# Where TensorE takes a pair's shared-expert down product within an even step

## The reference, cut to what matters

```python
x  = x + attention(layernorm(x), ctx)                  # Wq, Wk, Wv, Wout, bout
xn = layernorm(x)
logits = (xn @ Wr) / 16                                # 8 experts
idx = top_k(logits + rb, 2)                            # two experts for a token
w   = softmax(logits taken at idx)
routed = sum over idx of w * ((xn @ W1[e]) * silu(xn @ W3[e])) @ W2[e]     # H = 512
shared = ((xn @ Ws1) * silu(xn @ Ws3)) @ Ws2                               # H = 512
out = x + routed + shared
```

## Time and profile before

| what | value |
|---|---|
| median of 3 runs | 1096.32 us (1096.11 to 1097.06) |
| the profiled execution's own time | 1097.37 us |
| its span | 1095.3 us |
| mean granted TensorE clock | 0.985 |
| PE busy | 1061.2 us (97%) |
| DVE, POOL, ACT busy | 743.3 (68%), 705.3 (64%), 694.3 us (63%) |

### The profile page before, as it was taken

One profiled execution on the slowest core, in us unless ns is written; L12 is line 12 of the kernel. 1 busy time (PEld: TensorE's weight loads), 2 busy tenths in 40 slices (PEclk: granted clock), 3 DMA queues, 4 the chain that ended last, 5 costly groups with the idle time before them and its releaser, 6 DMA issues. The chain is left out here.

```text
span 1095.3 us, 25507 instructions
## 1 busy us (share of the span) xinstructions
PE 1061.2 (97%) x7342; PEld 929.1 (85%) x7342; DVE 743.3 (68%) x1940; ACT 694.3 (63%) x1649; POOL 705.3 (64%) x658
## 2 busy tenths in 40 slices
PE   6999999999999999999999899999999999999996
PEld 4788888888888888888887799999888888888886
DVE  5788888888888888888888676656443333433332
ACT  6888888888888888888886554332334343343442
POOL 4988889888988888898887556555033223332233
PEclk9999999999999999999998999889999999999998
DMA  8014431442144214421532295223473354333861
GB/s 247 17 41 131 139 103 37 139 139 94 45 139 139 86 53 139 139 78 62 178 103 94 77 304 185 81 76 127 147 217 56 58 137 87 56 56 62 269 176 15
DMA packets 83985, 124.06 MB, mean 113 GB/s; under 512 B 7904, under 2 KB 48080, under 8 KB 83920
## 3 DMA queue, kind: packets, MB, share of 16 engines
q1 hardware_dynamic: 63664, 99.86, 28.0%
q0 software_dynamic: 11760, 15.15, 7.7%
q10 hardware_dynamic: 8496, 8.22, 2.6%
HBM read 74.44 MB, written 49.68 MB: 113 GB/s over the span
## 5 line engine op out<-in xcount | busy, mean ns | idle before, releaser
L559 POOL TENSOR_TENSOR probs<-probs,first_rows 112x750 f32<-112x750 f32 x128 | 184.0, 1438 | 66.1 <-DVE first_rows L1019 64.9
L1801 POOL DMA_INDIRECT out<-stage,to_row x48 | 74.9, 1560 | 175.7 <-ACT stage L1853 114.6
L2082 DVE TENSOR_TENSOR hT_lo<-banks,hT_hi 128x512 fp32r<-128x512 f32 x63 | 43.6, 692 | 185.3 <-ACT hT_hi L1845 179.4
L753 ACT ACTIVATE probs<-banks,first_rows 112x375 f32<-112x375 f32 x256 | 145.8, 573 | 18.2 <-DVE first_rows L1006 16.0
L1006 DVE TENSOR_REDUCE first_rows<-banks 112x2 f32<-112x750 f32 x128 | 119.6, 934 | 26.1 <-PE banks L1391 24.4
L519 POOL TENSOR_TENSOR v_both<-v_raw,v_both 125x512 fp32r<-125x512 f32 x96 | 123.7, 1288 | 7.5
L1012 DVE TENSOR_TENSOR pT<-banks,pT 125x672 fp32r<-125x672 f32 x128 | 108.8, 850 | 18.2 <-ACT pT L744 17.0
L1405 PEld LDWEIGHTS banks<-pT,v_both 125*128 125x128 f32 x768 | 99.7, 192 | 17.4 <-issue 10.4
L1405 PE MATMUL banks<-pT,v_both 125*128 125x224 f32 x768 | 110.9, 280 | 2.2 <-DVE oT_lo L1037 1.7
L515 POOL TENSOR_TENSOR v_both<-v_raw,one 125x512 fp32r<-125x512 f32 x96 | 110.6, 1152 | 0.1
L1417 PE MATMUL banks<-ident,probs 112*125 112x112 f32 x768 | 107.6, 277 | 1.4 <-POOL probs L559 0.7
(11 more groups left out here) (286 smaller groups left out, 3066.6 us busy)
## 6 DMA issues: line engine op xcount, KB each, us to landing
w_split_scratch<-stage SPq DMA_DIRECT2D x16, 1536.0 KB, 6.6
ring<-w_split_scratch SPq DMA_DIRECT2D x16, 1536.0 KB
stage<-in_L_ffn_W SPq DMA_DIRECT2D x48, 256.0 KB, 3.0
ctx_in<-in_ctx SPq DMA_DIRECT2D x32, 376.0 KB, 3.8
xg<-x_sorted_scratch ACTq DMA_DIRECT2D x59, 136.0 KB
x_in<-in_x SPq DMA_DIRECT2D x16, 224.0 KB, 3.3
x_res<-in_x SPq DMA_DIRECT2D x32, 112.0 KB, 2.1
x_scratch<-x SPq DMA_DIRECT2D x32, 112.0 KB, 1.9
```

The costliest lines, as they stand in the source:

```text
L559: pool.tensor_tensor(probs[:, two, :], probs[:, two, :], inv_sum[:, 2 * s:2 * s + 2].rearrange("p (e o) -> p e o", o=1).to_broadcast([N, 2 ...
L753: act.activation(probs[:, h % 4, :], S_BANKS[0:N, e, 0:M], ACT.Exp, bias=neg_max[:, h:h + 1], accum_out=row_sum[:, h:h + 1]).then_inc(exp_ ...
```

## The change

On PE, in the even steps 2 to 24, `down_shared` moves from the end of the step to right behind `up1`, and so ahead of turn_block, turn_rows, router, ranks and the read of the ring's place. In step 26 it stays where it was. No instruction is added or removed, and no other engine's list changes.

```diff
                 if g < LAST:
                     up1(g)
+                if 2 <= g < SHARED_FIRST and g % 2 == 0:
+                    down_shared(g // 2 - 1)
                 j = g + 2 - SHARED_FIRST
                 if 0 <= j < BLOCKS:
                     turn_block(j)
@@
                     ring_off[n] = pe.value_load(ring_at[0:1, n:n + 1], min_val=0, max_val=2 * SLOT)
-                if 2 <= g <= SHARED_FIRST and g % 2 == 0:
+                if g == SHARED_FIRST:
                     down_shared(g // 2 - 1)
```

## The result

The change made the kernel slower: 1100.70 us in the median of 20 runs (1095.38 to 1104.26) against 1095.62 for the kernel before in 20 runs (1092.88 to 1101.71), a ratio of 1.0037 with a 95% interval of 1.0025 to 1.0048. Single executions of either kernel scatter by some 9 us, far more than the three runs shown before had suggested. The profiled execution took 1099.61 us with a span of 1097.5; its partner before took 1097.37.

What follows compares the result with a forecast made beforehand. PE, busy 1061.2 of 1095.3 us, was taken to bound the kernel. The terms -1.35 - 2.7 + 0.7 = -3.35 us took the median from 1096.32 to 1093.0 us, with an 8-in-10 range of 1089.5 to 1097.3.

Steps and rivals of the forecast that it cites:

- (a): PE's waits in steps 4, 10, 16 and 24: work resumes earlier with the new order, -1.35 us, bounds 0 and 3.25.
- my sign: Check in the changed profile: steps 4, 10, 16 idle about 0.7 us ahead of the down product, until ACT's `hi`.
- (b): Granted clock in the shared steps: three of five open falls after thin products remain, -2.7 us, bounds 0 and -7.9.
- Moved past: Steps 6 and 12: rows turned 2.9 us later, 0.8 us in hand where there were 3.7; given no term.
- (c): POOL's transfers run without a gap and hold PE's signals back in steps 6 and 12: +0.7 us, bounds 0 and +5.9.
- What POOL loses by the later start it has in hand: POOL's later start of slots and transfers costs nothing, since it waits for the next statistics after each chunk.
- The slower rival: Router of steps 7 and 13 waits behind held signals and the clock falls: 5.9 us more, 1098.9 us, chance 0.15.
- Its deciding point: Router waits if signals come free over 0.8 us after the turning's end; step 6 was put at 0.5 us.
- The clock rival: Clock falls as before in the shared steps, five falls making 9.4 us, (b) is 0: 1095.7 us, chance 0.26.

## Why the prediction was wrong, step by step

**(a) The waits, -1.35 us: failed.** The router's waits went, as forecast, but the down product's were 1.79, 1.01 and 0 us in steps 4, 10, 16, where my sum left 0.69, 0.45 and 0.34 (and my sign said 0.7 each): 2.8 us of idle time for 2.56. I took ACT's `hi` from the trace of before as a fixed time. It can itself stand behind a held signal. In the profile after, chunk 0's eight transfers ran in one train until 651.66, and the down product of step 4 started at 651.52. That train was not closed by the change, as shown above, so the 1.79 us are in part the draw of this execution. In step 24 the wait was 0.43 us, ahead of the down product, where it had been 0.69 us ahead of the turning; the separate run of that step found no gain.

**(b) The clock, -2.7 us: failed for the whole change, half right for the part it was argued for.** The mean granted clock is 0.9875 after (20 runs) and 0.9870 before (76 runs of the experiments, on four chips, whose means go from 0.9858 to 0.9876): no gain that can be told. With steps 4, 10, 16 alone it is 0.9895 (12 runs), against 0.9876 for the kernel before on the same chip (33 runs). Within kernels a run has some 0.83 us less for each 0.001 of granted clock (a fit over all runs, its scatter 1.6 us), so that part seems to have gained some 1.6 us by the clock, and as its time did not move, lost as much elsewhere; its profile has 1.1 us more idle time (7.4 against 6.3 in the stretch), and the rest is not shown. The full change did not keep the clock's gain: with the later turning alone it is 0.9868, and in the profile after three of the four falls stand right behind the waits of steps 4, 13 and 19, the fourth in step 5 behind thin products without a wait. That the falls of one trace are one draw held: they came at other places in every trace, and the runs scatter by 9 us. I wrote that one trace cannot tell and still built a sum with terms of 1 to 3 us on it.

**Moved past, the later turning of rows in steps 6 and 12, put at nothing: the step that decided the sign.** I counted 0.8 us in hand of the 3.7 there had been and gave it no term. Moved alone, these two steps cost 1.0045, some 5 us, and steps 4, 10, 16 alone cost nothing that can be told (1.0007). With the same closed trains, the kernel without the later turning has 1.0008 and the whole change 1.0037. My reading is that the slack let PE bear held signals: in step 13 they came 4.0 us after the turning, with 0.8 us in hand. Where no train is longer than five, the later turning costs nothing either (0.9905 against 0.9903). So in this change it took both, and I had priced them apart.

**(c) POOL's transfers close up, +0.7 us: right in kind and too small.** The mechanism is the one in the text: long trains hold PE's signals back, and breaking them up takes the loss away. In chunk 1 the six in a row came as forecast, and PE lost nothing there. The loss came from what I had not seen. I had trains of six; those of chunks 3 and 5 ran eight, since `hid` of two steps on was ready as well and the second gate was open too. I charged PE only for its short stops (0.45 us), not for what waits behind the signals: the router in step 13 and the ranks in step 19. And I looked for the closing only where ranks move; the later turning of steps 6 and 12 delays DVE's `take_chosen` and can close the next chunk's train too, as it did once in the run of that part alone. "What POOL loses by the later start it has in hand" was the wrong question, since it is not POOL's time that is short.

**The slower rival, 0.15, 1098.9 us: what happened.** In the profile it is at the place given, the router of step 13 with 1.25 us of idle time and a long fall of the clock behind it, but not in step 7, where DVE's `lo` was there 0.9 us ahead of the router. Its deciding point, signals that come free more than 0.8 us after the turning's end, was reached in step 13, with 708.14 - 704.12 = 4.0 us, since the train had eight transfers. It was the rival nearest to what happened, and it had the chance of 0.15. The measured ratio on the first median of 1096.32 us makes 1100.4 us, beyond the range of 1089.5 to 1097.3.

**The clock rival** had the clock's size right (b is 0 within what can be told), and its sum of 1095.7 us was wrong for lack of the later turning.

What stays open: by what path POOL's transfers hold PE's signals. The traces show engines that see a signal late and PE stopping before products, and the runs show that it goes away when no train is longer than three; they don't show where the signals wait. The table rests on one profile of each kernel, and the trains differ from one execution to the next, so how often each train closed in the timed runs is not known. The 1.0037 and the 1.0008 with the same trains were measured on different chips. Whether a pause shorter than those of the gates would do was not tried.

## What to carry to other kernels

When an engine is reordered, look at what each gate on another engine was holding apart, and at whether it will still be closed when its turn comes; here gates written for one order were open in the other. Slack that a move uses up is a price even where nothing waits in the trace; it is what bears the next late signal. A wait in a trace that ends with "issue" or an unknown releaser, on engines that had been served, is the first thing to explain, and its cure (one gate in each chunk moved by a step, 1% here) may be larger than the change in hand. Price terms of 1 to 3 us only against the scatter of many executions: three runs within 1 us said nothing of the 9 us in which twenty fell.

## What the runs showed of the hardware

- Indirect transfers issued by POOL back to back, 1.27 us apart, hold up the other engines' view of PE's results: ACT began 1.6 us after the last of eight, 4 us after PE's record of the turning ended. With all gates off the stretch has 11.1 us of idle time, with trains of 3 and 5 it has 2.7. With no more than three in a row, PE idled for 0.13 us in 132.67. So it is the transfers and not a busy POOL, which filled a tile in their place.
- The granted clock falls without idle time too: with no idle time in 133.99 us the stretch has 0.96. Idle time goes with a lower clock in one order of PE (2.7 to 11.1 us, clock 0.97 to 0.89), but not from kernel to kernel at large: 9.8 us with 0.94, 4.2 us with 0.99. In the profiles here the falls that lasted more than 6 us all began within 2 us or so of a wait of PE (in the kernel before behind the router's in steps 10 and 16).
